# One step of VectorE's order split in two: the low part of h, chunk 1, between the statistics of the next x and their aggregates

## What is computed

```
xn = layernorm(x)
q, k, v = split(xn @ Wqkv + bqkv)          # 256 features each
qp, kp = elu(q) + 1, elu(k) + 1
kv = kp^T v (per sequence);  k_sum = sum of kp over the tokens
z = layernorm(xn + (qp kv) / (qp . k_sum + 1e-6)) * g1 + b1
ffn = (silu(z @ Wg + bg) * (z @ Wu + bu)) @ Wd + bd      # 682 hidden features
s = layernorm(z + ffn) * g2 + b2
out = x + s * silu(xn @ ternary(W)^T)
```

## Time and profile before

| | |
|---|---|
| Median of 3 runs | 1211.54 us (1210.90 to 1212.32) |
| The profiled execution | 1212.66 us, its span 1211.0 us |
| Busy share of the span | TensorE 98%, VectorE 89%, ScalarE 79%, GpSimd 70% |
| Granted TensorE clock | 0.998 of full speed |
| DMA | 115.6 MB, mean 95 GB/s |

### The profile page before, as it was taken

One profiled execution on the slowest core, in us unless ns is written; L12 is line 12 of the kernel. 1 busy time (PEld: TensorE's weight loads), 2 busy tenths in 40 slices (PEclk: granted clock), 3 DMA queues, 4 the chain that ended last, 5 costly groups with the idle time before them and its releaser, 6 DMA issues.

```text
span 1211.0 us, 24021 instructions
## 1 busy us (share of the span) xinstructions
PE 1190.9 (98%) x7550; PEld 1070.2 (88%) x7550; DVE 1082.2 (89%) x2467; ACT 953.3 (79%) x1557; POOL 841.7 (70%) x994
## 2 busy tenths in 40 slices
PE   8999999999999999999999999999999999999997
PEld 6889998989988999989999988999988899888886
DVE  6988999999999999999999999999999999777765
ACT  7787888878888887888878888778797788867753
POOL 3443787767787776787767777667776677766676
PEclk9999999999999999999999999999999999999999
DMA  7213432334432334432234432234332343222201
GB/s 217 74 50 88 123 106 70 88 105 123 123 104 72 87 106 123 118 103 78 87 106 122 121 104 74 74 120 123 108 96 63 101 123 105 70 71 61 76 22 35
DMA packets 137524, 115.61 MB, mean 95 GB/s; under 512 B 12340, under 2 KB 122294, under 8 KB 137399
## 3 DMA queue, kind: packets, MB, share of 16 engines
q1 hardware_dynamic: 137398, 114.08, 32.2%
HBM read 67.38 MB, written 46.67 MB: 94 GB/s over the span
## 4 chain that ended last, share of the span: by engine, by line
PE 86%; DVE 7%; issue 2%; ACT 2%; DMA 1%; POOL 1%; SPq 0%; DVEq 0%; POOLq 0%; ACTq 0%
PE bank L1271 61%; PE d_bank L1271 17%; PE xk_bank L1271 7%; DVE st L922 1%; DMA z_turned<-xa 1%; DMA xa<-z_turned 1%; DVE rz L1054 1%; PE bank L1285 1%; DVE bank L1095 0%; DVE h_l L1105 0%; ACT rz L695 0%; DVE zT_l L1085 0%; POOL norm L569 0%; ACT hs L695 0%; DVE kp L1014 0%
## 5 line engine op out<-in xcount | busy, mean ns | idle before, releaser
L1271 PE MATMUL bank<-zT_h,wgu_h 128*128 128x512 f32 x704 | 275.6, 391 | 1.1 <-DVE rz L1054 1.0
L1271 PE MATMUL bank<-zT_l,wgu_h 128*128 128x512 f32 x704 | 275.7, 392 | 0.0
L1271 PE MATMUL bank<-zT_h,wgu_l 128*128 128x512 f32 x704 | 275.4, 391 | 0.0
L695 ACT ACTIVATE rz<-rz,norm 128x256 f32<-128x256 f32 x252 | 140.5, 596 | 57.7 <-DVE norm L1131 57.1
L569 POOL TENSOR_TENSOR norm<-ve,consts 128x4 f32<-128x4 f32 x64 | 72.9, 1139 | 153.6 <-DVE ve L933 153.5
L1271 PE MATMUL d_bank<-wd_h,h_h 128*128 128x256 f32 x640 | 179.2, 280 | 0.1
L1271 PE MATMUL d_bank<-wd_h,h_l 128*128 128x256 f32 x640 | 179.0, 280 | 0.0
L1271 PE MATMUL d_bank<-wd_l,h_h 128*128 128x256 f32 x640 | 179.0, 280 | 0.0
L1095 DVE SCALAR_TENSOR_TENSOR bank<-bank,hb,hs 128x512 f32<-128x512 f32 x160 | 117.9, 754 | 54.0 <-ACT hs L695 42.3
L695 ACT ACTIVATE h_h<-bank 128x512 fp32r<-128x512 f32 x160 | 95.8, 599 | 80.9 <-DVE bank L1095 80.5
L1271 PEld LDWEIGHTS bank<-zT_l,wgu_h 128*128 128x128 f32 x704 | 132.1, 188 | 28.8
(11 more groups left out here) (163 smaller groups left out, 3576.3 us busy)
## 6 DMA issues: line engine op xcount, KB each, us to landing
xq<-in_L_attn_x_dram SPq DMA_DIRECT2D x32, 512.0 KB, 6.0
xa<-in_L_attn_x_dram SPq DMA_DIRECT2D x31, 512.0 KB, 3.9
out_dram<-rz SPq DMA_DIRECT2D x31, 512.0 KB, 5.0
z_turned<-xa SPq DMA_DIRECT2D x120, 128.0 KB, 3.3
xa<-z_turned SPq DMA_DIRECT2D x30, 512.0 KB, 4.1
turned<-xa SPq DMA_DIRECT2D x108, 128.0 KB, 2.5
xa<-turned SPq DMA_DIRECT2D x27, 512.0 KB, 3.9
rz<-in_L_attn_Wg_dram SPq DMA_DIRECT2D x1, 640.0 KB, 5.2
```

Source lines behind the costliest of these rows:

```text
L695: return eng.activation(out_, in_, func, **kw).then_inc(S[name], 1)
L1271: ins = eng.matmul(dst, left, right, start=first and n == 0, stop=last and n == len(pairs) - 1, **kw)
```

## The change

`aggregate(0, g)` leaves `a_stats` and becomes a step of its own, `a_aggregate`. In the steady order it stands behind `h_low 1`, right ahead of `q_aggregate`. In the fill it stands right behind each `a_stats` from group 1 on (group 0 has a form of its own, `first_stats`, that is not touched). In the lists for the last iteration there is neither.

```diff
--- before.py
+++ after.py
@@ -99,7 +99,7 @@
 VECTOR_STEPS = steps("""
     xk_low 0, zT_low 0, k_add 0, zT_low 1, kv_bias 0, kv_bias 1, kv_low 0, kv_low 1, ffn_rows 0,
     ffn_rows 1, k_add 1, last_stats 0, attn 0, last_shift 0, attn 1, attn 2, attn 3, h_rows 0, k_max 0,
-    h_low 0, h_rows 1, a_stats 0, h_low 1, q_aggregate 0, h_rows 2, a_norm 0, x_turn 0, attn_norm 0,
+    h_low 0, h_rows 1, a_stats 0, h_low 1, a_aggregate 0, q_aggregate 0, h_rows 2, a_norm 0, x_turn 0, attn_norm 0,
     k_max 1, h_low 2, k_low 0, q_elu 0, z_turn 0, q_elu 1, q_low 0, k_low 1, h_rows 3, h_rows 4,
     q_low 1, h_low 3, x_low 0, h_rows 5, x_low 1, h_low 4, h_low 5""")
 GPSIMD_STEPS = steps("""
@@ -143,13 +143,13 @@
     x_high 5 0, x_high 5 1, z_rows 0 0, z_rows 0 1, z_rows 0 2, z_rows 0 3, silu_tern 0 1, q_high 1 1,
     xn_high 5 0, xn_high 5 1""")
 FILL_VECTOR = fill("""
-    a_stats 0 0, a_stats 0 1, a_norm 0 0, a_norm 0 1, setup_k_low 0 0, xT_low 0 0, a_stats 1 0,
+    a_stats 0 0, a_stats 0 1, a_norm 0 0, a_norm 0 1, setup_k_low 0 0, xT_low 0 0, a_stats 1 0, a_aggregate 1 0,
     a_norm 1 0, setup_bk 0 0, xT_low 0 1, k_add 0 0, setup_q_low 0 0, xT_low 1 0, k_add 0 1, k_max 0 0,
-    a_stats 2 0, setup_bq 0 0, k_max 0 1, k_add 1 0, a_norm 2 0, xT_low 1 1, q_elu 0 0, k_max 1 0,
-    q_low 0 0, k_add 1 1, setup_gu_low_0 0 0, xT_low 2 0, k_max 1 1, a_stats 3 0, k_add 2 0, xT_low 2 1,
-    a_norm 3 0, setup_gu_low_1 0 0, q_elu 0 1, k_max 2 0, xT_low 3 0, k_add 2 1, a_stats 4 0, k_max 2 1,
+    a_stats 2 0, a_aggregate 2 0, setup_bq 0 0, k_max 0 1, k_add 1 0, a_norm 2 0, xT_low 1 1, q_elu 0 0, k_max 1 0,
+    q_low 0 0, k_add 1 1, setup_gu_low_0 0 0, xT_low 2 0, k_max 1 1, a_stats 3 0, a_aggregate 3 0, k_add 2 0, xT_low 2 1,
+    a_norm 3 0, setup_gu_low_1 0 0, q_elu 0 1, k_max 2 0, xT_low 3 0, k_add 2 1, a_stats 4 0, a_aggregate 4 0, k_max 2 1,
     setup_v_low 0 0, k_add 3 0, q_low 0 1, xT_low 3 1, a_norm 4 0, setup_d_bias 0 0, k_max 3 0,
-    k_add 3 1, a_stats 5 0, k_max 3 1, xT_low 4 0, setup_ternary 0 0, q_elu 1 0, xk_low 0 0, xT_low 4 1,
+    k_add 3 1, a_stats 5 0, a_aggregate 5 0, k_max 3 1, xT_low 4 0, setup_ternary 0 0, q_elu 1 0, xk_low 0 0, xT_low 4 1,
     k_add 4 0, kv_bias 0 0, kv_bias 0 1, a_norm 5 0, kv_low 0 0, kv_low 0 1, x_turn 5 0, k_max 4 0,
     k_add 4 1, attn 0 0, k_low 4 0, k_max 4 1, setup_ternary_parts 0 0, attn 0 1, attn 0 2, attn 0 3,
     q_aggregate 0 0, k_low 4 1, attn_norm 0 0, setup_d_tail 0 0, x_low 5 0, q_elu 1 1,
@@ -956,7 +956,6 @@
                 eng.wait_ge(s_xa[g % 2], 16 * ((g + 1) // 2))
                 for t in range(TILES):
                     stats(0, g, t, xa[:, g % 2, t, :])
-                aggregate(0, g)
 
             def a_norm(g, p=0):
                 if g == 0:
@@ -1258,7 +1257,7 @@
                     "q_low": (q + 1, q_low), "k_max": (a, k_max), "k_low": (a, k_low), "kv_bias": (q, kv_bias),
                     "kv_low": (q, kv_low), "xk_low": (q, xk_low), "setup_v_low": (a, setup_v_low), "ffn_rows": (last, ffn_rows),
                     "h_rows": (f, h_rows), "attn": (q, attn), "h_low": (f, h_low), "a_norm": (a + 1, a_norm), "x_turn": (a + 1, x_turn), "x_low": (a + 1, x_low),
-                    "q_aggregate": (q, lambda g, _: aggregate(1, g)), "last_stats": (last, last_stats),
+                    "a_aggregate": (a + 1, lambda g, _: aggregate(0, g)), "q_aggregate": (q, lambda g, _: aggregate(1, g)), "last_stats": (last, last_stats),
                     "attn_norm": (q, attn_norm), "z_turn": (q, z_turn), "last_shift": (last, last_shift),
                     "end_rows": (last, end_rows), "xT_low": (a + 1, xT_low)})
 
```

## The result

The changed kernel takes 1217.07 us, the median of 6 runs (1215.99 to 1217.93), the kernel before 1211.8 us (6 runs, 1210.90 to 1212.32). The ratio is 1.0044, with a 95% interval of 1.0032 to 1.0057: slower by 5.3 us. The prediction was 1217.6. The profiled execution of after took 1216.9 us around a span of 1215.2, at a granted clock of 0.997.

A forecast was written before the change was run, and what follows sets the result against it. The prediction took VectorE and TensorE as bounds of nearly the same length. Its terms, mainly 16 common rounds at +0.43 us, summed to +6.0 us on 1211.54, rounded up to 1217.6 us; range 1209.2 to 1222.

The forecast's parts named there:

- What bounds: Steady rounds: VectorE and TensorE bound nearly equally; TensorE's plain round is 35.79 us, the shortest rounds 35.71.
- The first gain: TensorE's Q chunk 1 no longer waits for `h_low 1`: alone worth at most 2.0 us.
- The chain from `ve` to `last_add 3`: `ve` 0.61 us later delays GpSimd; `q_low 1` meets `last_add 3` and ends at 17.60 instead of 17.17: 0.43 us.
- The other branch: Seven rounds where GpSimd got ahead of `k_max 1`: `last_add 3` ends at 16.97, `q_low 1` at 17.52.
- What was costed at nothing: SP's later transfers and ScalarE's later `zT_high` and `x_res`: no cost, or up to 0.2 us a round, 5 in all.
- hidden: `h_low 2` ends at 8.67 instead of 8.39, before TensorE wants it at 9.06 for U 3: no cost.
- 6.9 + 0.7 - 0.7 - 0.2: 16 common rounds +6.9 us; two with the other `k_max` +0.7; gaps before `h_rows 5` -0.7; TensorE once ahead -0.2.
- The last `a_stats`, +0.4: The last `a_stats`, at 997.76 us, was to add 0.4 us to the sum.
- C: No change: phase differs by round, or `last_offset 1` doesn't hold `a_norm`; 1211 to 1213 us, chance 0.13.
- B: Faster: `last_add 3` late by 0.57 to 0.7 us, no round held, TensorE bounds; 1208.0 us, chance 0.14.
- d: GpSimd's slide: a held `q_low 1` costs about this much, back to nothing at 0.65 to 0.7 us, then again.
- D: Worse: `q_low 1` 0.56 us late everywhere, or U 3 waiting for `h_low 2` adds to the round; 1220.5 us, chance 0.11.

The follow-up runs named there:

- after with one clear: The changed kernel, with GpSimd also clearing 256 unused `ksum` columns between `z_g1 3` and `sum_k 1`: 1210.15 us, ratio 1.0001.
- before with two clears: The kernel before, with GpSimd also clearing 200 unused `ksum` columns twice between `z_g1 3` and `sum_k 1`: 1210.52 us, ratio 1.0004.
- the split alone: The kernel before, with `a_aggregate` a step of its own but right behind `a_stats`, so the instruction order is unchanged: 1211.25 us, ratio 0.9998.
- the clears of 40 and 190: The kernel before, with GpSimd also clearing 40 and 190 unused `ksum` columns between `z_g1 3` and `sum_k 1`: 1217.94 us, ratio 1.0056.
- `last_offset 1` moved: The changed kernel, with GpSimd's `last_offset 1` put ahead of `a_rstd`: 1221.53 us, ratio 1.0080.

## Why the prediction was right

**What bounds.** It held that VectorE and TensorE are bounds of nearly the same length. With `q_low 1` free and no wait for Q chunk 1 (after with one clear) 12 of the 18 plain rounds take 35.66 to 35.71 us; TensorE's own round is therefore at most that, and the 35.79 read from the chain held 0.1 us of waits. The trace of before could have told it: its shortest round is 35.68 us, not the 35.71 that the prediction calls the shortest.

**The first gain.** The wait at Q chunk 1 was to be worth at most 2.0 us. It went as expected. Whether it is worth anything apart from the rest of the change can't be told; together with that rest, but with `q_low 1` free, it comes to nothing: on one chip after with one clear has the ratio 1.0001 (0.9992 to 1.001), before with two clears, which has the old order and an equally free `q_low 1`, 1.0004 (0.9995 to 1.0013).

**The chain from `ve` to `last_add 3`.** Every station that it gives is within 0.04 us of the trace: `h_low 1` 1.32 (1.31), `a_rstd` 2.57 (2.56), `last_offset 1` 3.56 (3.55), first `xn` to 4.45 (4.43), `k_max 1` 7.38 (7.38), gate 2 8.74 (8.74), `k_low 0` 8.59 unheld (8.58, 0.67 us), `last_offset 3` 11.92 and `q_low 0` 11.94 (11.93 and 11.94), `last_add 3` 16.32 to 17.05 (16.32 to 17.07), `q_low 1` to 17.60 (17.61). One thing differs: `a_norm` was released at 3.61, not 3.65, which the held `xn` hides. VectorE's lateness ends in the idle time before `h_rows 3`, which starts at 15.12 (15.11), as told. The other branch, `last_offset 2` ahead of `k_max 1`, came in 6 of 25 rounds (7 before), with `h_low 2` ending at 9.28 and `q_low 1` at 17.51 to 17.54, as told.

**What was costed at nothing.** SP's transfers and ScalarE: after with one clear the output and the next xq leave 1.1 us late, and nothing is lost. `h_low 2` for U 3: "hidden" holds in the common round; after a long `k_max 1` it isn't, the wait is up to 0.68 us. In the changed kernel those rounds are no longer than the others (36.06 against 36.12), because VectorE's lateness covers it. Where `q_low 1` is free it shows: 36.02 in place of 35.67 in two such plain rounds of after with one clear, and 35.99 to 36.02 in three of after with `q_low 1` ahead of `h_rows 3`. So "hidden" was right only because another term was larger.

**The sum.** Round by round, the 18 whose `q_low 1` was short before are 6.6 us longer (0.22 to 0.47 each); the same terms of the prediction, 6.9 + 0.7 - 0.7 - 0.2, give 6.7. The six whose `q_low 1` was long are 1.7 us shorter, predicted 1.1; 0.9 of it is one round, at 855.78, of 35.72 us. There `zT_low`'s second operation started at 878.93, 0.03 us ahead of GpSimd's `xn_low` at 878.96, and took 0.67 us; in the round shown above GpSimd was first (584.43) and it took 1.18. It is the same pair of engines at another place, which the prediction didn't follow. Nor is that round a sign of the change: in the kernel with the split alone, which has the order of before, it takes 35.60 us, and 36.63 in before. The last `a_stats`, +0.4, didn't come: the stretch behind it is 0.30 us shorter. Predicted +6.0, in the profiled executions 4.2 to 4.9, in the medians 5.3. That 1217.6 and 1217.07 lie so close is in part luck: the same change measured +6.5 us beside the clears of 40 and 190 (1217.54 and 1210.99), and the profiled executions of before and of the split alone, the same instructions in the same order, differ by 1.0 us in their spans (1211.0 and 1210.0). The range has a slip too: 1209.2 is called the lower edge of C, and C begins at 1211.

**The rivals.** B named its condition, `last_add 3` late by 0.57 to 0.70, and the two kernels with d of 0.60 and 0.68 meet it: one `q_low 1` in 25 is held in the latter (1.04 us, the round at 230), and in the former those after a long `k_max 1` and one more (0.93 us, the round at 886). But its price was wrong. It gave 1208.0 us, 3.5 below the 1211.54 of before, 3.2 of it for six long `q_low 1` that go; the medians on one chip are equal. The profiled executions do differ by 3.3 us (1209.41 with one clear, 1212.66 before), but that is no measure: they weren't taken side by side (the median of before is 1211.8 where the result was measured and 1210.23 beside the kernel with one clear), and the profiled execution of before lies 0.9 us above the median of its kernel, the other 0.7 below. Nor were six long ones too many for a usual execution: the split alone, with the order of before, has six again (1.07 to 1.30 us). Its 24 rounds take 875.90 us, those of after with one clear 873.95, and a part of what `q_low 1` gives back there is taken by the rounds of 36.02 us. Why nothing of the rest is left in the medians stays open. C's grounds are both out by the trace: `last_offset 1` holds `a_norm` in every round, and `q_low 1` is long in 24 of 25 rounds, only at 231.70 does it take 0.82 us. D's price, the full 0.56 us in every round, is the kernel with `last_offset 1` moved, at +10 us: the upper end given for the unknown; its other ground, U 3's waits for `h_low 2`, came five times and made no round of after longer.

**The page of the Trainium skill** (SBUF — State Buffer, Who interferes with whom) says that the pair of ports that VectorE and GpSimd share is locked for a whole instruction by whoever starts first. For full-width pairs this trace agrees: `q_low 1` ends 0.55 us behind the neighbour that is ahead of it, or takes 0.68 to 0.73 us where it is first, and 0.02 us decide; the held `xn` ends 0.15 us behind its neighbour. For the four-element `q_rstd` it doesn't: it ran 1.20 us, and the last three `xn` beside it took 0.40 each, and the 1220 us that the rule taken whole would give did not come.

What stays open: what decides a race within some 0.02 us, as at `k_max 1`, which differs from round to round in both kernels, and how often each outcome comes in executions that weren't profiled. No version here beats the kernel before by more than the interval; `q_low 1` ahead of `h_rows 3` in it is the nearest (0.9984 to 1.0002).

## What to carry to other kernels

Where two engines exclude each other in some pairs of instructions, what an edit costs is read at the pairs that stand behind the last idle time, from the phase in which the two arrive, and not at the wait that the edit removes. Here VectorE lost its half microsecond in its own idle time; GpSimd, which had next to none on that stretch, kept it and handed it back to VectorE behind that idle time. Before taking a loss for granted, shift the other engine by a cheap, harmless instruction: if more work makes the kernel faster, as it did here, it was the phase. In this kernel a place ahead of the idle time was the right one for the instruction that is held.

## What the runs showed that I had not expected

- A clear of 256 columns on GpSimd takes 0.31 us and moves what follows by 0.25 us; a second one that waits for the first adds some 0.17 us of its own: two of 200 columns moved the rest by 0.60 us, of 40 and 190 by 0.43.
- The price as a function of phase has a cliff: at d = 0.43 the kernel loses 5 to 7 us, at 0.60 nothing, at -0.15 ten.
- Waits of the busiest engine can follow the round rather than set it: those of TensorE's weight loads put down to issue rose from 5.5 us (10 times) to 9.6 us (28 times) in after, and are 5.1 us (8 times) with the one clear, at nearly unchanged work.
